# Laying a first batch's own chain between the steps that prepare weights

## What is computed

```python
# layer 0, per batch (8 heads of 16 channels)
q = Wq0 @ y + bq0;  k = Wk0 @ y + bk0;  v = Wv0 @ x + bv0
attn = softmax(q_h @ k_h.T / sqrt(128))
o = Wo0 @ (attn @ v) + bo0 + x
h = (o - mean(o)) * rsqrt(var(o) + 1e-5) * gn_w + gn_b
# layer 1
q = lora(h, Wq, Aq, Bq);  k = lora(y, Wk, Ak, Bk);  v = lora(y, Wv, Av, Bv)
# lora(x, W, A, B) = x @ W + 2.0 * (x @ A @ B)
out = h + lora(softmax(q @ k.T / sqrt(32)) @ v, Wo, Ao, Bo)
```

## Time and profile before

| what | us |
|---|---|
| median of 3 runs | 1371.63 |
| lowest and highest | 1371.59, 1376.06 |
| the profiled execution | 1379.2 |
| its span | 1377.4 |
| TensorE busy | 1335.9 (97%) |
| VectorE, ScalarE, POOL busy | 929.4, 825.3, 160.9 |

### The profile page before, as it was taken

One profiled execution on the slowest core, in us unless ns is written; L12 is line 12 of the kernel. 1 busy time (PEld: TensorE's weight loads), 2 busy tenths in 40 slices (PEclk: granted clock), 3 DMA queues, 4 the chain that ended last, 5 costly groups with the idle time before them and its releaser, 6 DMA issues.

```text
span 1377.4 us, 24115 instructions
## 1 busy us (share of the span) xinstructions
PE 1335.9 (97%) x7135; PEld 1052.0 (76%) x7135; DVE 929.4 (67%) x2075; ACT 825.3 (60%) x2924; POOL 160.9 (12%) x129
## 2 busy tenths in 40 slices
PE   6899999999999899999999999999999999999998
PEld 5777888888878788888888888767666676766666
DVE  5666666666665677777767776587676777666665
ACT  4466655555550677777757776676655566665441
POOL 6533333222210000000000000400000000000000
PEclk9999999999999999999999999999999999999999
DMA  7455556666655677777777777997989889897772
GB/s 187 148 180 190 191 188 193 218 218 218 227 175 179 199 217 234 231 224 228 219 233 228 219 223 246 284 257 226 248 243 264 243 251 248 237 256 228 226 222 77
DMA packets 198915, 300.45 MB, mean 218 GB/s; under 512 B 30658, under 2 KB 97828, under 8 KB 198276
## 3 DMA queue, kind: packets, MB, share of 16 engines
q1 hardware_dynamic: 198788, 298.92, 73.1%
HBM read 213.88 MB, written 84.93 MB: 217 GB/s over the span
## 4 chain that ended last, share of the span: by engine, by line
PE 84%; ACT 7%; DVE 3%; issue 3%; DMA 2%; SPq 1%; ACTq 0%; DVEq 0%
PE bank L660 24%; PE bank L697 21%; PE bank L556 11%; PE bank L715 7%; PE bank L748 5%; PE bank L759 4%; ACT lora_aT_kv L901 2%; PE bank L501 2%; PE bank L631 2%; ACT x_hi L893 1%; DMA q_stack<-lse_dram 1%; ACT kv_sb L936 1%; PE bank L581 1%; PE bank L586 1%; PE bank L646 1%
## 5 line engine op out<-in xcount | busy, mean ns | idle before, releaser
L962 ACT ACTIVATE bank<-bank,negs 128x128 f32<-128x128 f32 x1024 | 349.5, 344 | 202.9 <-DVE negs L1216 202.6
L660 PE MATMUL bank<-hT,wq 128*128 128x512 f32 x1488 | 392.8, 401 | 3.1 <-DVE hT L1176 3.1
L697 PE MATMUL bank<-wo,op 128*128 128x512 f32 x1344 | 347.3, 396 | 2.9 <-DVE h_blk L1300 2.0
L660 PEld LDWEIGHTS bank<-hT,wq 128*128 128x128 f32 x1488 | 264.9, 189 | 50.4 <-DVE hT L1176 4.1
L697 PEld LDWEIGHTS bank<-wo,op 128*128 128x128 f32 x1344 | 250.1, 189 | 55.2 <-DVE op L1271 2.4
L1211 DVE TENSOR_REDUCE maxes<-bank 128x4 f32<-128x512 f32 x256 | 175.6, 686 | 127.1 <-PE bank L715 122.4
L979 ACT ACTIVATE probT<-bank 128x512 f32<-128x512 f32 x256 | 151.8, 605 | 107.0 <-PE bank L748 103.1
L962 ACT ACTIVATION_READ_ACCUMULATOR bank<-bank,negs 128x1 f32 x1024 | 212.8, 208 | 0.0
L556 PE MATMUL bank<-wkv_hi,yT 128*128 128x512 f32 x512 | 204.9, 421 | 0.3 <-POOL wkv_lo L1486 0.3
L715 PEld LDWEIGHTS bank<-k_stack,q_stack 96*128 96x128 f32 x1024 | 151.1, 192 | 20.7 <-DMA k_stack<-k_dram 5.0
L715 PE MATMUL bank<-k_stack,q_stack 96*128 96x128 f32 x1024 | 148.3, 268 | 4.2 <-DMA k_stack<-k_dram 3.9
(11 more groups left out here) (167 smaller groups left out, 1631.6 us busy)
## 6 DMA issues: line engine op xcount, KB each, us to landing
q_stack<-q_dram SPq DMA_DIRECT2D x384, 128.0 KB, 3.3
q_dram<-q_part SPq DMA_DIRECT2D x64, 512.0 KB, 4.5
q_stack<-q_dram SPq DMA_DIRECT2D x128, 256.0 KB, 3.7
y_in<-in_ctx SPq DMA_DIRECT2D x32, 512.0 KB, 4.5
x_in<-in_x SPq DMA_DIRECT2D x32, 512.0 KB, 5.2
h_dram<-h_out SPq DMA_DIRECT2D x32, 512.0 KB, 2.6
h_in<-h_dram SPq DMA_DIRECT2D x32, 512.0 KB, 4.5
k_stack<-k_dram SPq DMA_DIRECT2D x128, 128.0 KB, 3.2
```

The source lines that it names most:

```text
L660: m = pe.matmul(bank(u % 2).rearrange("p (a n) -> p a n", a=2), wq[:, block, part, c, :], hT[(group + 1) % 2][:, :, of, c, :], start=c == ...
L697: mm = pe.matmul(out_bank(pair, m), op[m][:, of, c, :], wo[m][w][:, c, :], start=c == 0 and of == 0 and w == 0, stop=c == GROUP - 1 and of ...
L962: act.activation(part, part, ACT.Exp, bias=negs[:, n % RING, j:j + 1], scale=SCORE1, accum_out=sums[:, score_column(k), g, j:j + 1]).then_ ...
```

## The change

- On ACT the sum of the first y (`sum_y(0)`) stands ahead of all else and writes its by-product into `x_hi`; its scale of the bias (`scale_bias`) is a step of its own, later.
- The chain of batch 0 (turning the gram, t1, scores, softmax, n1) and `turn_y(1)` stand between the eight steps of the weights on PE, ACT and DVE; the list of the small banks has the same order.
- The q factors are turned in b = 1 instead of 0 and the o factors in b = 6 instead of 1 (batches 2 and 7, counted from one). POOL prepares each one batch ahead.
- POOL's copy of B and the subtraction are cut into two halves each.

```diff
+        STACKED = {1: "q", 6: "o"}
+        FIRST_CHAIN = {3: ("gram", "gram"), 4: ("t1", "t1"), 5: ("s", "s_sb"), 7: ("n1", "n1")}
...
@@ tensor_program
                 if n == 0:
                     gram_products(0)
+                if n == 2:
+                    turn_gram(0)
+                    turn_layer0()
+                if n == 3:
+                    t1_product(0)
                 if n == 4:
-                    turn_layer0()
+                    score_product(0)
+                    turn_y(1)
                 if n >= 3:
-                    kv_products(0, (n - 3,), early=True)
-            for b in range(B):
...
+                    kv_products(0, (n - 3,))
+                if n == 6:
+                    n1_product(0)
+            kv_products(0, (5, 6))
+            mix_product(0)
+            kv_products(0, (7,))
+            mixed_x(0)
+            for b in range(1, B):
+                gram_products(b)
...
-                if b < 2:
-                    stack_lora("qo"[b])
+                if b in STACKED:
+                    stack_lora(STACKED[b])
@@ scalar_program
+            sum_y(0)
             stack_lora("kv")
...
+                if n == 2:
+                    turn_layer0()
                 if n == 4:
-                    turn_layer0()
+                    act.wait_ge(S["bqk"], 1)
+                    scale_bias(0)
+                if n == 5:
+                    round_yT(1, 0)
+                    softmax0(0)
+                if n == 6:
+                    round_yT(1, 1)
                 if n + 1 < NC:
                     prep_round(n + 1)
...
+            split_x(0)
+            evacuate_n1(0)
+            round_mix(0)
+            evacuate_kv(0)
+            sum_y(1)
+            scale_bias(1)
@@ vector_program
+                if n == 2:
+                    finish_gram(0)
+                if n == 3:
...
+                    evacuate_t1(0)
+                if n == 4:
+                    softmax0_begin(0)
+                if n == 5:
+                    rest_yT(1, 0)
+                    softmax0_end(0)
+                if n == 6:
+                    rest_yT(1, 1)
+            split_mix(0)
@@ gpsimd_program
-                pool.tensor_scalar(lora_b[m][:], lora_b3[m][:], 1.0, None, ALU.mult).then_inc(stack, 1)
+                for half in range(2):
+                    of = slice(half * BANK, (half + 1) * BANK)
+                    done = pool.tensor_scalar(lora_b[m][:, of], lora_b3[m][:, of], 1.0, None, ALU.mult)
+                done.then_inc(stack, 1)
...
-                if b < 2:
-                    stack_lora("qo"[b])
+                if b + 1 in STACKED:
+                    stack_lora(STACKED[b + 1])
```

More of the change, by code:

```diff
@@ L540, in gram_products, with kv_products @@
                 m.then_inc(S["gram_mm"], 1)
[L543 to L545 removed]
+            def kv_products(b, chunks):
                 for c in chunks:
[L547 to L548 removed]
                     if c == 0 and b:
```

106 lines of the change are left out of this document (47 added, 59 removed).

## The result

| | before | changed |
|---|---|---|
| median, runs | 1373.36 us, 4 | 1384.42 us, 4 |
| lowest and highest | 1371.59, 1376.06 | 1384.00, 1386.04 |
| the profiled execution, its span | 1379.2, 1377.4 | 1386.04, 1384.2 |

The changed kernel takes 1.0081 times as long, with an interval of [1.0059, 1.0103]: slower by 0.8%. The forecast was slower by 0.3% (1375.9), and the range ended at 1380.0. The medians differ by 11.1 us, the two profiled executions by 6.8: that of before lies 5.8 us above the median of its four runs, that of the changed kernel 1.6.

A forecast was written before the change was run, and what follows sets the result against it. TensorE was taken to bound ordinary batches, with idle time only before 48.84 us and VectorE setting mixed_x(0). Terms -0.85 + 3.8 + 1.1 + 0.3 = +4.35 us on 1371.63 gave 1375.9 us; range 1370.0 to 1380.0.

The forecast's parts named there:

- gram(2) after 52: Sign of being wrong: gram(2) starting before 49 or after 52 us, or batch 6 lasting under 14 us.
- Sum of y ahead: Start of the first batch: the sum fits into ScalarE's idle time before its first copy, so it costs nothing.
- The chain among the weight pieces: First batch: mixed_x(0) starts near 29.6 instead of 31.43, 1.8 us gained, with VectorE setting this.
- late layer-0 weights: Rival, chance 0.20, shared with an early clock fall: columns landing at 17.0 make the sum +5.75; with both, +6.9 us.
- Giving back in b = 1: Batch 1: POOL is never idle and TensorE waits nearly 2 us for it; 1.35 of the 1.8 us are left.
- End of b = 1: End of batch 1: the product waits for both halves of q, 0.5 us; 0.85 us of gain left at gram(2).
- Batch 6: Batch 6: with the o factors turned there, its product comes at 113.40 instead of 109.57, 3.8 us lost.
- The 1.1 for the clock: Batch 6: after about 2.7 us idle, mixed_x's three pairs run at the low clock, 1.1 us lost.
- the rival with 0.15: The clock spares b=6, or also b=1: +3.25 or +2.2 us, thus 1374.9 or 1373.8; chance 0.15.
- POOL in b = 5: Late in batch 5: POOL's o stack lies beside mix_split(5) and lengthens it by 0 to 1.4 us, taken as 0.3.

The follow-up runs named there:

- bias_later: The changed kernel with VectorE's two instructions on the scores' bias one step later, behind t1: 1378.23 us, 1.0033.
- warm: The changed kernel with eleven extra 512-column products on TensorE, six ahead of the turn of layer 0, five ahead of the score: 1379.91 us, 1.005.
- y_later: The changed kernel with the turn of the second y behind the seventh weight piece on TensorE instead of ahead of it: 1380.91 us, 1.0048.
- mended: The changed kernel with the edits of bias_later and pool_later, and the o turns behind mixed_x(6), their rests in b = 7: 1372.5 us, 0.998.
- early_loads: The changed kernel with the layer-0 loads issued from ScalarE's queue at the program's start instead of SP's: 1383.59 us, 1.0074.
- mended_y_later: The mended kernel plus the turn of the second y behind the seventh weight piece on TensorE: 1372.11 us, 0.9989.
- pool_later: The changed kernel with POOL's preparation of the q factors behind the power of batch 0 instead of ahead of x_lo(1): 1379.11 us, 1.0037.

## Why the prediction was wrong

The sign was right and the size was not. The prediction's own sign of being wrong, gram(2) after 52, came (55.69). By its own steps:

*Sum of y ahead:* right. The sum ran before the first copy, and the first product started at 11.65 against 11.75.

*The chain among the weight pieces:* this step failed, by 5.15 us at `mixed_x(0)` (29.6 forecast, 34.75 measured). It splits at three instructions of the same trace. In its own terms, `score_bias` and att were priced too low, the turn was priced for a clock that stays high, and the columns were taken to land too early.
- The score, 20.0 forecast, came at 22.38. The columns were taken as landed at 15.6 and landed at 16.6: the fifth product stands at 18.24 where 17.2 was forecast, 1.0 us. This agreement hides two errors that cancel: 15.6 and the 1.05 of turns and biases make 16.65 and not 17.2, and turns and biases took 1.58, as the clock fell within them. The rival "late layer-0 weights" had this at its place, priced 1.4. Another 1.1 us is `score_bias`, taken at its length of before (0.35) and measured at 1.45; bias_later shows it. The last 0.3 lie in the other links, the fifth product at the lower clock (0.80) among them.
- The seventh product, 22.2 forecast, came at 26.36, another 1.8. The turn was taken at 1.03 "if the clock stays high", and it didn't: the stretch from 17 to 23 us was granted 0.52, the lower level. Score, turn and chunk took 3.98 us instead of 2.2. warm, with the high clock, won 1.5 to 2.1 between the score and `mixed_x(0)`, y_later, with the turn behind the seventh product, 1.3 to 2.0.
- The seventh and eighth merges took 1.0 more: 26.36 to 30.41 instead of 3.05 us. att was blocked for 0.5 and the product ahead of the merge was slow. From the end of the eighth merge to `mixed_x(0)` it was 4.34 us, and 4.35 was forecast.

So the old durations were laid into a new order, and two kinds didn't carry over: VectorE's short instructions, once they came beside POOL's subtractions, and TensorE's, once it worked at the lower clock early. What brings this fall stays open. It came in eight of the nine traces with the early chain and no fillers. In the changed kernel it followed a wait of 1.37 us for the columns. In bias_later and mended it came before such a wait, and in early_loads, by the lengths, without one. Only mended_y_later, where TensorE didn't wait for the columns either, and warm with its fillers were spared. The prediction gave both falls of the clock and late columns 0.20 as a rival and capped it at +6.9 with 1.1 us for a fall, taken from three pairs of matmuls; a fall that lasts 10 us costs more, and its signs stood in rows of before (0.58 at 24 us, turn 1.91). VectorE's blocking had been priced in b = 5 and, for `mix_split(0)`, as a wait for the end of x_lo, which came out (1.02 us), and not for `score_bias` and att, which the chain had moved beside POOL's rests of the pieces. The Trainium skill (SBUF — State Buffer, who interferes with whom) says of a VectorE instruction with two SBUF inputs that it contends with a GpSimd one that reads SBUF; the rows at 20.53 and 33.58 agree. The one at 29.02 was held too, although its second input is only one number a row, so that this sentence doesn't cover it. That the short links on VectorE are held for as long as the POOL subtraction lasts could be read from the row of before at 44.40; the same price at `score_bias` would have put the score about 1 us later.

*Giving back in b = 1:* right in kind and size. POOL without a gap, the power ending at 44.53, VectorE waiting at `norm_scale`, TensorE's wait 2.56 ("nearly 2"). From `mixed_x(0)` to n1(1) it was 11.54 us, forecast 11.2. pool_later shows the cause.

*End of b = 1:* right. The product waits for the second VectorE piece of the q factors (1.96). n1(1) to gram(2) took 9.40 us where 9.74 was forecast, but part of this is luck: up to `mixed_x(1)` it was 0.90 us longer than before where 0.5 was forecast, and two of the three pairs of `mixed_x(1)` ran at the high clock (0.63 and 0.69, before 1.05), where no change of clock was forecast. The fall came at 54.8, with the third pair (1.05).

*Batch 6:* right: 3.89 us measured, 3.8 forecast, and its idle time of 2.48 against 2.7, though in two pieces (0.87 and 1.61) and not on end. The 1.1 for the clock didn't come in this profile (b = 7 even took 11.34 us instead of 11.80), so that b = 6 and 7 lost 3.4 and not 4.9: in this term the rival with 0.15 was right. It did come in four of the seven traces with the same waits; what decides isn't shown. The Trainium skill's advice to keep idle gaps short (TensorE: Matmul & The Clock Gate, why this matters for your kernels) thus agrees with four traces of seven.

*POOL in b = 5:* 0.3 forecast, nothing measured. `mix_split(5)` took 0.29 us, and from `mixed_x(4)` to `mixed_x(5)` it was 11.81 us against 11.82. The 0.7 us between gram(2) and `mixed_x(5)` lie all in batch 2, whose first 2.5 us run at the low clock (before, 0.2). Another 0.6 came between `mixed_x(7)` and the first projection, where 0 was forecast; no row here explains it.

Steps add to 9.0 at the first projection. The medians differ by 11.1. The missing 2 us aren't explained by the profiles; the three traces with the same first batch differ by as much at `mixed_x(0)`, and the profiled execution of before was itself 5.8 us above its median. Laying the sum on the median of three runs (of four it is 1373.36; later runs of before on three chips have medians of 1373.9 to 1374.56) added 1.7 us to the miss. The forecast of `mixed_x(0)`, 29.6, is about what the chain gives in mended_y_later (29.31), where `score_bias` took 0.60, the turn stands behind the seventh product, and the clock stayed high (the turn took 1.03).

## What to carry to other kernels

When a chain is moved between other work, price each short instruction by what runs beside it at the new place, not by its old length; POOL's program has to be laid out beside VectorE's for that. Give a turn or copy that isn't wanted soon the place behind the bounding product rather than ahead of it: over two batches eight turns cost 3.4 us ahead of `mixed_x` (4.8 where the clock fell) and 1.15 behind. And where a change makes the early work of a stage thinner on TensorE, price all that follows at the lower clock as a case of its own, with a real chance: here it came in eight of nine traces.

## What the runs showed of the hardware

- How exactly VectorE's blocking repeats: `score_bias` took 1.44 to 1.47 us in all seven programs that kept it beside POOL's rest and 0.35 where it was moved behind it; `mix_split(1)` took 1.25 to 1.87 beside POOL's subtraction and 0.29 without. An instruction with one matrix input and one number a row (att, 29.02) lasted 0.78, which had not been expected. POOL's own instruction wasn't lengthened (1.26 to 1.29 us in the seven), although by the profile `score_bias` started 0.03 or 0.04 us ahead of it.
- Same waits, other clock: behind 0.87 and 1.61 us of waits a pair of matmuls took 0.62 us in three traces and 1.05 in four.
- The clock column of a profile can read high where the lengths say low: in early_loads it reads 1.00 throughout the first batch, yet the turn of y took 1.92 us, as at 0.50 in the changed kernel.
- The last of the eleven layer-0 transfers, issued at 12.95, was waited for until 16.66. In the one trace where they were issued at the program's start from another queue, y landed 0.8 us later.
- The identical first batch started `mixed_x(0)` at 32.71, 33.40 and 34.75 in three programs.
